# An attention and feed-forward layer: context stored as 256 plain rows, value products of two steps next to each other, and a new order of work inside a round

## The chip, the cores and the metric

The kernel runs on one core of one Trainium2 chip. The metric is the device time in microseconds (us). Three runs of the kernel before took 2249.22, 2251.18 and 2252.72 us; the median is 2251.18 us.

The core has a matrix engine (PE, with PEld for its weight loads), a vector engine (DVE), a scalar engine (ACT), a general engine (POOL) and a sequencer that issues transfers (SP). Each has its own queue and runs it in order; semaphores tie them together.

## The reference

One layer of a transformer: batch 2, sequence 2048, width 256, 16 heads of 16, relative position embeddings clipped at distance 64, then a feed-forward part of width 704 whose activations and weights are rounded to a 4-bit grid in blocks of 16.

```python
B, S, D, H, R = (2, 2048, 256, 16, 64); HD = 16
dist = jnp.clip(idx[None, :] - idx[:, None], -R, R) + R
pe_k, pe_v = rel_emb_k[dist], rel_emb_v[dist]
q, k, v = qkv[0], qkv[1], qkv[2]              # from layernorm(x) @ W_qkv + b_qkv
score = einsum('bhqd,bhkd->bhqk', q / sqrt(hd), k) + einsum('bhqd,qkd->bhqk', q / sqrt(hd), pe_k)
attn = softmax(score)
ctx = einsum('bhqk,bhkd->bhqd', attn, v) + einsum('bhqk,qkd->bhqd', attn, pe_v)
x = x + ctx @ W_out + b_out
xq = fp4(layernorm(x)); h = silu(xq @ fp4(w_gate).T) * (xq @ fp4(w_up).T)
x = x + fp4(h) @ fp4(w_down).T
```

## The kernel before

**Stages.** `projections` makes queries, keys and values, `attention` does the rounds, `ffn_weights` transposes the weights of the last part, and `ffn` does the output projection and the feed-forward part, 32 tiles of 128 tokens.

**A round.** The attention part is 32 rounds (`iteration`): 8 groups of 4 heads times 4 blocks of 512 queries. A round has 16 steps. Each step has a string in `ORDER`, and every engine walks the same strings and does its share of each letter:

- `S`: one half of a score unit, 128 keys by 512 queries of one head, into one of 4 PSUM banks (`psS`). PE makes it (steps 0 and 1: `near_half`, with four transposes L925 and four products L932; later steps: `far_half` L943), ACT takes the exponential (L1084, L1089).
- `M`: one product of the search for each query's maximum, one or two rounds ahead (PE L845, into one of 3 banks of `psA`); DVE reduces it (L1139). There are 64 in a round. The last three steps of a round already hold those of the round after next (`AHEAD`, 11 of them).
- `V`: the value products of one step (`far_values` L863): four heads, each on its own 32 columns of the array, fp32, summed in `psC`. In step 2 it is `band_values` (L955). A `V` works on the step before it; the last step's is done at the start of the next round.
- `P`, `F`: relative positions for the values (L968, then DVE L1179, then L980). `P` needs POOL's `mix_band` (L798, L804), which starts when `band_values` is done.
- `R`, `X`: the relative scores of the next round (PE L852, ACT L1076, DVE L1144, POOL `widen_rel` L790). When the fourth is widened, SP writes them out and reads them back skewed (`rel_skew`, then `rel_near`).
- `T`: the negated maxima of the next round are transposed (L871), ACT copies them (L1068), POOL cuts them in three (`cut_shift` L778 to L784) and SP puts them beside the queries (`queries<-shift`, L717). In a round at an end of the sequence (qb 0 and 3) POOL first clears an edge of `rel_near` (L772).
- `D`, `B`: the end of the last round. ACT copies `psC` (`copy_context` L1056, at the start of step 1), PE transposes the sums (`denominators` L879), DVE inverts them (L1160), ACT widens the inverses (L1063), PE transposes them back (`turn_back` L887, four transposes), DVE multiplies (`normalise` L1167) and SP stores the context in 32-row strips per head (L722).

**Slots.** `probs` has four slots: the exponentials of two steps. The exponential of step s waits until the value product of step s-2 is done.

**After the rounds.** The value bias and the first row of the relative values are not in the values; `ffn_weights` works them, and the output bias, into spare rows of `w_out_rows` (taps: DVE L1714 to L1718, PE L1748, DVE L1726). In `ffn` each tile's output projection is four fp32 products (`project` L1432), each recorded twice. PE's order for tile n is gate and up product of n+1, down product of n-1, projection of n+5, transposes of x of n+2 and of h of n. DVE follows the strings `ODD` and `EVEN` with the operations of h (`H`), of x (`X`, one pair of tiles every two tiles) and of the output (`Y`).

Of the kernel before, what the change touches and what calls it, by code (L numbers as in the profile page):

```python
# [30 lines left out]
P = 128  # L31
# [24 lines left out]
VWIDE = 32  # L56

# [59 lines left out]
def projections(nc, c, x, w_qkv, b_qkv, rel_k, rel_v, dr, io):  # L117
# [13 lines left out]
    with ExitStack() as ctx:  # L131
        def sb(name, shape, dt=F32):
            return ctx.enter_context(nc.sbuf_tensor(name, shape, dt))

        (w_in, x_in, b_in, passed, ln_stats, ln_var, ln_std, ln_rstd, ln_done, p_dve, xt_ready, xt_copied,
# [3 lines left out]
            "w_in x_in*2 b_in passed ln_stats ln_var ln_std ln_rstd ln_done p_dve xt_ready xt_copied "  # L139
# [17 lines left out]
        prt = sb("rel_prt", [HD, 3, P], BF16)  # L157
        rv = sb("rv_rows", [P, 2, HD])
# [72 lines left out]
        def _(sp):  # L231
# [22 lines left out]
            sp.dma_start(w[:], w_qkv.rearrange("(c p) n -> p c n", p=P)).then_inc(w_in, 16)  # L254
            with nc.allow_non_contiguous_dma("small tables, once"):
                sp.dma_start(bcol[:], b_qkv[0:2 * D].rearrange("(t p) -> p t", p=P)).then_inc(b_in, 16)
                sp.dma_start(relT[:], rel_k.rearrange("r d -> d r")).then_inc(k_dma, 16)
            sp.dma_start(rv[:, 0, :], rel_v[0:1, :].broadcast_to([P, HD])).then_inc(k_dma, 16)
# [75 lines left out]
        def _(dve):  # L334
# [32 lines left out]
            def values(n):  # L367
# [3 lines left out]
                for i in range(CH):  # L371
                    dve.wait_ge(v_ready, n * (CH // 2) + i // 2 + 1)
                    src = psV[:, i, :].rearrange("p (h d) -> p h d", h=H)
                    if i:
                        v.tensor_copy(vheads[:, t0 + CH * j + i, :, 0:HD], src).then_inc(v_taken, 1)
                    else:
                        v.tensor_copy(vheads[HALF:P, t0 + CH * j, :, 0:HD], src[HALF:P]).then_inc(v_taken, 1)
                        v.tensor_copy(vheads[0:HALF, t0 + CH * (j + 1) % KT, :, 0:HD], src[0:HALF]).then_inc(v_taken, 1)

            def relative_tables():  # L380

                dve.wait_ge(k_dma, 16 * 4)
                ch.mark(v.tensor_sub(vd[:, 0, :], rvt[:], rv[:, 0, :]))
                ch.link(v.tensor_sub(vd[:, 1, :], rvt[:], rv[:, 1, :]))
                dve.sem_inc(k_rel, 1)
# [9 lines left out]
            def masks():  # L395
# [3 lines left out]
                ch.link(v.tensor_reduce(c.head[:], c.ident[:].rearrange("p (h c) -> p h c", h=HG)[:, :, 0:HD], AX.X, ALU.add))  # L399
# [13 lines left out]
            dve.wait_ge(b_ready, 2)  # L413
            for n in range(N):
# [73 lines left out]
class Dram:  # L488


    def __init__(self, nc):
# [7 lines left out]
        self.ctx = d("ctx_d", [B * KT, P, HG, P])  # L499


class Consts:
    def __init__(self, nc, ctx):
# [6 lines left out]
        self.head = sb("head_rows", [P, HG])  # L510
# [31 lines left out]
RSTEPS = (4, 5, 6, 7)  # L542

ORDER = (
    "MSMVMMSMSMMSM", "SMSMMSMSDM", "SMMSSMVMSMB", "VSMSSMMS",
    "SMSMSSMVRM", "MSMSMSSXMRV", "XSSMMSSMVRM", "SMSMSSMVRXM",
    "SSMSMXSVP", "MSVSMSMSM", "SMSSSMVF", "MMSMSVMSS",
    "SMMSMSVMS", "SSMSVMST", "MMSSMSVMSMM", "SSMVMSSM",
)
RATE = tuple(x.count("M") for x in ORDER)  # L550
# [12 lines left out]
def score_slots():  # L563
# [3 lines left out]
    def add(*key):  # L567
        slots[key] = len(slots)
# [4 lines left out]
    for it in range(LAST + 1):  # L573
        for step in range(STEPS):
            half = 0
            for kind in ORDER[step]:
# [3 lines left out]
                elif kind == "R" and it < LAST:  # L580
                    add("R", it + 1, RSTEPS.index(step))
# [18 lines left out]
def emptied(*key):  # L600

    return SCORE[key] + 1 + SBANKS

# [38 lines left out]
def attention(nc, c, dr, io, fw):  # L642
    with ExitStack() as ctx:
        def sb(name, shape, dt=F32):
# [5 lines left out]
         shift_ready, ctx_copied, rden_wide,  # L650
# [4 lines left out]
            "shift_ready ctx_copied rden_wide "  # L655
# [4 lines left out]
        probs = sb("probs", [P, 4, 2, NQ])  # L660
# [5 lines left out]
        rwide = sb("rden_wide", [P, NQ])  # L666
# [4 lines left out]
        rden = sb("rden", [P, NQ])  # L671
# [25 lines left out]
        def _(sp):  # L697
# [21 lines left out]
            def store_context(g, qb):  # L719

                wait_alone(sp, passed, small_taken, taken("B", g * QB + qb))
                sp.dma_start(ctx_rows(g, qb), rden[:].rearrange("p (i t) -> p i t", i=CH)).then_inc(ctx_out, 16)  # L722

            def iteration(g, qb, before=None, last=False):
# [14 lines left out]
                if it == 1:  # L739
                    sp.wait_ge(w_set, 4)  # L740
# [4 lines left out]

            def ctx_rows(g, qb):
                b, gg = g // NG, g % NG
                return dr.ctx[bass.ds(b * KT + qb * CH, CH), :, gg, :].rearrange("i p t -> p i t")
# [12 lines left out]
            wait_alone(sp, passed, ctx_out, 16 * (GRP * QB + 1))  # L761
# [29 lines left out]

# [1008 lines left out]
```

## Time and profile before

| | |
|---|---|
| median of three runs | 2251.18 us |
| the profiled execution | 2251.05 us |
| its span, first to last instruction | 2249.2 us |
| PE busy | 2174.0 us (97%) |
| DVE busy | 1868.9 us (83%) |
| ACT busy | 1349.4 us (60%) |
| POOL busy | 676.4 us (30%) |
| mean granted clock of PE | 0.979 of full |

Stages by the trace: projections to about 123 us; the first maxima to 171; the rounds to about 1873; the last context to 1877; the weights to 1890; the feed-forward part to 2249. PE's busy share is near full in both long stages. The share alone does not say whether PE sets the pace: the matrix products overlap, and their ends are modelled. What an engine really takes is read from the distance between the starts of two instructions when nothing was waited for.

### The profile page before, as it was taken

The page shows a single profiled execution, that of the slowest core. Times are in us where ns is not written, and L with a number is a line of the kernel's source. Part 1 is how long each engine was busy: PE and PEld are TensorE (multiplying, and loading weights), DVE is VectorE, ACT ScalarE, POOL GpSimd, SP SyncE. Part 2 cuts the span into 40 slices and gives each one's busy share as a digit, 9 for nine tenths or more (in the row PEclk, how much of TensorE's full clock was granted, in tenths as well). Part 3 has the DMA queues.
Part 4 walks back from the last instruction along what each step waited for, and adds up shares of the span by engine and source line. Part 5 has one row for each costly group of instructions (what it writes and reads, how often), then busy time and mean ns, then how long its engine had stood idle before and what let it go on. Part 6 is the DMA issues. An engine that isn't in the chain of part 4 may idle for free. (4 is left out here: it accounts for less than half of the span.)

```text
span 2249.2 us, 50086 instructions
## 1 busy us (share of the span) xinstructions
PE 2174.0 (97%) x20396; PEld 1139.1 (51%) x20396; DVE 1868.9 (83%) x3408; ACT 1349.4 (60%) x2544; POOL 676.4 (30%) x484
## 2 busy tenths in 40 slices
PE   7989999999999999999999999999999996999998
PEld 3524444554444444444444444545444443677775
DVE  6787888888888888888888888888888833899997
ACT  3406766767677777676776766766677773233332
POOL 5503333333333333333333333333333330011111
PEclk9958999999999999999999999999999998999999
DMA  5743433343333333433443333343333221111100
GB/s 162 192 115 92 137 98 88 102 106 91 98 103 98 88 97 98 114 105 102 110 112 98 98 98 98 96 105 98 92 89 88 81 81 63 38 57 54 50 33 17
DMA packets 275178, 210.74 MB, mean 94 GB/s; under 512 B 16642, under 2 KB 266116, under 8 KB 274820
## 3 DMA queue, kind: packets, MB, share of 16 engines
q1 hardware_dynamic: 273796, 203.34, 32.9%
q0 software_dynamic: 1152, 4.19, 0.6%
q8 instruction: 161, 2.64, 0.5%
q14 instruction: 69, 0.57, 0.1%
HBM read 113.35 MB, written 93.34 MB: 92 GB/s over the span
## 5 line engine op out<-in xcount | busy, mean ns | idle before, releaser
L1139 DVE TENSOR_REDUCE amax<-psA 128x1 f32<-128x512 f32 x2048 | 1297.2, 684 | 203.6 <-PE psA L845 190.3
L1089 ACT ACTIVATE probs<-psS 128x512 f32<-128x512 f32 x1792 | 943.3, 609 | 337.4 <-PE psS L943 333.0
L845 PE MATMUL psA<-keys,queries 96*128 96x512 bf16 x2048 | 737.4, 390 | 2.0 <-DVE amax L1139 2.0
L943 PE MATMUL psS<-queries,keys 102*128 102x512 bf16 (+7 forms) x2176 | 586.1, 342 | 0.7
L863 PE MATMUL psC<-probs,vals 128*32 128x512 f32 (+7 forms) x4352 | 475.7, 524 | 3.9 <-ACT probs L1089 2.2
L798 POOL TENSOR_TENSOR band_probs<-band_probs,side 128x2048 f32<-128x2048 f32 x64 | 288.9, 4535 | 494.2 <-PE psC L955 494.2
L845 PEld LDWEIGHTS psA<-keys,queries 96*128 96x128 bf16 x2048 | 190.7, 98 | 336.6 <-DVE amax L1139 224.3
L943 PEld LDWEIGHTS psS<-queries,keys 102*128 102x128 bf16 (+1 forms) x2176 | 203.2, 98 | 213.4 <-ACT probs L1089 46.8
L1084 ACT ACTIVATE band_probs<-psS 128x512 f32<-128x512 f32 x256 | 153.6, 601 | 131.9 <-PE psS L932 131.8
L863 PEld LDWEIGHTS psC<-probs,vals 128*32 128x32 f32 (+1 forms) x4352 | 89.2, 102 | 197.0 <-ACT probs L1089 111.8
L1452 PE MATMUL psG<-w_gate_up_T,f_xqT 128*128 128x352 f32 x512 | 161.9, 471 | 0.5 <-ACT f_xqT L1508 0.5
L925 PE MATMUL psS<-ident,rel_near 128*128 128x128 f32 x1024 | 156.4, 275 | 0.0
L925 PEld LDWEIGHTS psS<-ident,rel_near 128*128 128x128 f32 x1024 | 129.6, 142 | 35.4 <-ACT band_probs L1084 1.1
L804 POOL TENSOR_TENSOR band_probs<-band_probs 128x2048 f32<-128x2048 f32 x32 | 145.2, 4537 | 5.7 <-POOL band_probs L798 2.9
L1391 POOL TENSOR_TENSOR f_hq<-f_h_grid,f_h_scale 128x704 f32<-128x704 f32 x32 | 44.4, 1388 | 305.3 <-DVE f_h_grid L1627 305.3
L1452 PEld LDWEIGHTS psG<-w_gate_up_T,f_xqT 128*128 128x128 f32 x512 | 97.6, 196 | 51.1 <-issue 4.5
L932 PE MATMUL psS<-queries,keys 99*128 99x128 bf16 (+1 forms) x1024 | 100.5, 220 | 9.0 <-DMA queries<-shift 8.7
L1076 ACT COPY rel_scores<-psS 128x512 f32<-128x512 f32 x128 | 75.5, 593 | 52.0 <-PE psS L852 52.0
L778 POOL CAST shift<-shift_res 32x128 bf16<-32x128 f32 x32 | 9.1, 284 | 310.8 <-ACT shift_res L1068 310.8
L772 POOL MEMSET rel_near<- 128x256 f32 x16 | 5.1, 317 | 303.1 <-DMA rel_near<-rel_skew 303.1
L1472 PE MATMUL psD<-w_down_T,f_hqT 128*128 128x256 f32 x384 | 89.9, 385 | 1.9 <-ACT f_hqT L1516 1.9
L790 POOL COPY rel_scores<-rel_scores 128x512 f32<-128x512 f32 x128 | 78.0, 638 | 36.1 <-ACT rel_scores L1076 36.1
(164 smaller groups left out, 1923.7 us busy)
## 6 DMA issues: line engine op xcount, KB each, us to landing
rel_skew<-rel_scores SPq DMA_DIRECT2D x32, 2048.0 KB, 9.1
rel_near<-rel_skew SPq DMA_DIRECT2D x64, 1024.0 KB, 8.1
keys<-k_ring SPq DMA_DIRECT2D x48, 256.0 KB, 5.7
queries<-q_parts SPq DMA_DIRECT2D x192, 64.0 KB, 2.4
ctx_d<-rden SPq DMA_DIRECT2D x32, 256.0 KB, 2.3
ctx_in<-ctx_d SPq DMA_DIRECT2D x16, 512.0 KB, 3.9
q_parts<-parts SPq DMA_DIRECT2D x16, 384.0 KB, 3.1
k_ring<-parts SPq DMA_DIRECT2D x12, 384.0 KB, 3.3
```

Source lines behind the costliest of these rows:

```text
L798: p.tensor_mul(both, both, c.side[:, e, None, :].broadcast_to([P, APAIRS, P])).then_inc(side_cut, 1)
L804: p.tensor_add(band[:, 0].rearrange("p h u q -> p (h u q)"), band[:, 0].rearrange("p h u q -> p (h u q)"), band[:, 1].rearrange("p h u q - ...
L845: t.matmul(small("M", m, n), qs[0:NR, qb, h, u * P:(u + 1) * P], keys[0:NR, par, h, c0:c0 + NQ], start=True, stop=True).then_inc(small_rea ...
L863: ins = t.matmul(psC[32 * h:32 * h + v.shape[1], q0:q0 + k], v, probs[:, n % 4, h % 2, o:o + k], start=False, stop=False, skip_group_check ...
L925: t.matmul(bank[:, u * P:(u + 1) * P], near[:, h * CH + u, e, :], c.ident[:], start=(u == 0), stop=False, is_transpose=True, skip_group_ch ...
L932: ins = t.matmul(bank[:, u * P:(u + 1) * P], keys[0:nr, par, h, c0:c0 + P], qs[0:nr, qb, h, u * P:(u + 1) * P], start=False, stop=(u == CH ...
L943: ins = t.matmul(bank[:, o:o + k], keys[0:nr, par, h, c0:c0 + P], qs[0:nr, qb, h, q0:q0 + k], start=True, stop=True, skip_group_check=True)
L1084: ins = a.activation(band[:, e, 2 * c2 + half].rearrange("p u q -> p (u q)"), src, ACT.Exp)
L1089: ins = a.activation(probs[:, n % 4, half], src, ACT.Exp)
L1139: v.reduce_max(amax[:, pair, k:k + 1], small("M", m, n), AX.X).then_inc(small_taken, 1)
L1452: ins = t.matmul(psG[:, half, 0:GU], xqT[:, m % 4, cc, :], wgu[:, cc, half * GU:(half + 1) * GU], start=(cc == 0), stop=(cc == 1))
L1472: ins = t.matmul(psD[:, 0:D], hqT[:, m % 2, f, :], wd[:, f, :], start=(f == 0), stop=(f == FT - 1))
```

## The change

- **Order.** `ORDER` is a new table. Value products are no longer tied to the step before: `value_order` lists them, two (steps 14 and 15) go over to the next round, and `VV` puts two next to each other. `probs` has eight slots.
- **Context.** DVE divides straight from the transposed sums (`scale`), POOL adds the part of the last relative row (`add_ends`), PE turns the result back with two transposes, DVE copies it (`take_turned`), and SP stores plain rows, 16 per head, in two transfers. `widen_inverses` is gone. ACT's copy has a letter of its own, `C`.
- **Biases.** The value bias and the first relative row are added to the values in `projections`; the output bias is added to x by POOL in `ffn` (`add_bias`). The taps are gone.
- **Projection.** Two products per tile instead of four.

```diff
 ORDER = (
-    "MSMVMMSMSMMSM", "SMSMMSMSDM", "SMMSSMVMSMB", "VSMSSMMS",
-    ... twelve more
+    "MMVVMSMMSMMSMMSC", "SMSMDSMSM", "SMSSSMM", "SSMVMSMSM",
+    ... twelve more
 )
+PROBS = 8
+CARRIED = 2
+def value_order(it):
+    left = [(it - 1, step) for step in range(STEPS - CARRIED, STEPS)] if it else [None] * CARRIED
+    return left + [(it, BAND_STEPS - 1)] + [(it, step) for step in range(BAND_STEPS, STEPS - CARRIED)]
...
+            def add_ends(it):                                  # POOL, between cut_shift and mix_band
+                wait_alone(pool, passed, small_taken, taken("D", it))
+                p.tensor_mul(ended[:], scaled[:, :, HD + 1:HD + 2].broadcast_to([P, APAIRS, HD]),
+                             c.ends[:, None, :].broadcast_to([P, APAIRS, HD])).then_inc(ends_added, 1)
+                ...
+                p.tensor_add(rows[:], scaled[:, :, 0:HD], ended[:]).then_inc(ctx_rows_ready, 1)
...
             def turn_back(it):
-                pe.wait_ge(rden_wide, it + 1)
+                pe.wait_ge(ctx_rows_ready, it + 1)
                 slot_free("B", it)
-                for u in range(CH):
+                for j in range(2):
                     ...
-            pe.sem_inc(pv_done, 2)
+            pe.sem_inc(pv_done, PROBS // 2)
...
-            def widen_inverses(it):
...
-            def invert(it):
+            def scale(it):
                 ready("D", it)
+                v.reciprocal(rcol[:], sums[:, :, HD]).then_inc(inverted, 1)
+                ...
+                v.tensor_mul(scaled[:], sums[:, :, 0:HD + 2], rcol[:, :, None].broadcast_to([P, APAIRS, HD + 2])).then_inc(small_taken, 1)
-            def normalise(it):
-                v.tensor_mul(rden[:], ctxs[:], small("B", it)).then_inc(small_taken, 1)
+            def take_turned(it):
+                v.tensor_copy(turned[:].rearrange("p j t -> p (j t)"), small("B", it)[:, 0:2 * P]).then_inc(small_taken, 1)
...
+            def add_bias(p):                                   # POOL in ffn
+                pool.wait_ge(r_in[k], 16 * (p // 2 + 1))
+                nc.gpsimd.tensor_add(both, both, bo[:, None, :].broadcast_to([P, 2, D])).then_inc(res_ready, 1)
+            add_bias(0)
+            add_bias(1)
             for n in range(NT):
+                if n % 2 == 0 and n // 2 + 2 < NP:
+                    add_bias(n // 2 + 2)
                 pool.wait_ge(hs_ready, n + 1)
...
-                for g in range(NG):
-                    ins = t.matmul(psO[...], cx[:, p % 2, half, g, :], wo[:, g, :], ...)
+                for cc in range(D // P):
+                    ins = t.matmul(psO[...], cx[:, p % 2, half, cc, :], wo[:, cc, :], ...)
...
-            pe.wait_ge(w_copied, 3 * KD)                       # ffn_weights
+            pe.wait_ge(w_free, KD)
```

PE's queue in the middle of a round before, around step 8 (`psA<-keys,queries` is an M, `psS<-queries,keys` an S, `psC<-probs,vals` a V, `tv` is P):

```order
L943 MATMUL psS<-queries,keys 128x512
L863 MATMUL psC<-probs,vals 32x512 x4
L968 MATMUL psA<-band_probs,tv 32x32 x64
L845 MATMUL psA<-keys,queries 128x512
L943 MATMUL psS<-queries,keys 128x512
L863 MATMUL psC<-probs,vals 32x512 x4
L943 MATMUL psS<-queries,keys 128x512
```

The same work now, in step 11:

```order
L886 MATMUL psA<-keys,queries 128x512
L984 MATMUL psS<-queries,keys 128x512
L886 MATMUL psA<-keys,queries 128x512
L904 MATMUL psC<-probs,vals 32x512 x8
L1009 MATMUL psA<-band_probs,tv 32x32 x64
L984 MATMUL psS<-queries,keys 128x512
L886 MATMUL psA<-keys,queries 128x512 x2
```

A block of 32-column products (V, P, F) that stood apart now often holds two or three of them: `x8` is two value products in a row. The positions moved from step 8 to step 11, the fold from step 10 to 12. In a whole round there were 15 such blocks and there are 11: by steps, before 0, 2, 3, 4, 5, 6, 7, 8 (V P), 9, 10 (V F), 11, 12, 13, 14, 15; now 0 (V V), 3, 4, 6, 7, 8 (V V), 10 (V V), 11 (V V P), 12 (F V), 13, 15. The band's products moved from step 2 to 3, `D` stayed in step 1 and `B` went from step 2 to 4; the last `R` went from step 7 to 8, `T` from the end of step 13 to the middle of 14. `AHEAD` is now 9.

POOL's queue for one round before (cut of the shift, mixing of the band, widening of the relative scores):

```order
L784 TENSOR_TENSOR shift<-shift_res,shift 32x128
L798 TENSOR_TENSOR band_probs<-band_probs,side 128x2048 x2
L804 TENSOR_TENSOR band_probs<-band_probs 128x2048
L790 COPY rel_scores<-rel_scores 128x4x128 x4
L778 CAST shift<-shift_res 32x128
```

and now:

```order
L811 TENSOR_TENSOR shift<-shift_res,shift 32x128
L823 TENSOR_TENSOR ctx_ends<-ctx_scaled,rel_v_ends 128x256
L828 TENSOR_TENSOR ctx_rows<-ctx_scaled,ctx_ends 128x256
L836 TENSOR_TENSOR band_probs<-band_probs,side 128x2048 x2
L842 TENSOR_TENSOR band_probs<-band_probs 128x2048
L817 COPY rel_scores<-rel_scores 128x4x128 x4
L805 CAST shift<-shift_res 32x128
```

Two operations on the context of the round before stand ahead of the mixing.

## Rows read from the trace of the kernel before

**Rows 1.** The page, part 1: busy time, share of the span, instructions of each engine.

```profile
PE 2174.0 (97%) x20396; PEld 1139.1 (51%) x20396; DVE 1868.9 (83%) x3408; ACT 1349.4 (60%) x2544; POOL 676.4 (30%) x484
```

**Rows 2.** Windows: stretch, its length, busy time (instructions) by engine, clock, DMA share, GB/s.

```profile
600.00:1600.00 1000.00, 996.90 (x10978) 485.96 (x10977) 869.73 (x1503) 699.26 (x1333) 336.78 (x226) 1.00 0.37 100
1827.00:1873.00 46.00, 42.14 (x504) 18.96 (x504) 1.64 (x3) 34.10 (x66) 14.12 (x4) 0.96 0.03 7
2000.00:2200.00 200.00, 199.74 (x866) 149.84 (x865) 192.98 (x405) 67.07 (x110) 26.50 (x20) 1.00 0.14 45
```

**Rows 3.** Source line L871, once a round: ns min/median/max, first and last start.

```profile
L871 PE MATMUL psS<-ident,negm x32: 272/273/421, 171.6 to 1820.4; 128*32 128x128 f32 x32
```

**Rows 4.** Timeline of PE, two stretches of one round: start us, us, line, operation.

```profile
1005.59 1.05 PE L863 MATMUL psC<-probs,vals 128*17 128x512 f32 x8
1006.46 1.42 PE L968 MATMUL psA<-band_probs,tv 128*32 128x32 f32 x128
1007.81 0.39 PE L845 MATMUL psA<-keys,queries 96*128 96x512 bf16 x1
1008.03 0.38 PE L943 MATMUL psS<-queries,keys 99*128 99x512 bf16 x1
1008.34 1.05 PE L863 MATMUL psC<-probs,vals 128*17 128x512 f32 x8
1009.33 0.39 PE L943 MATMUL psS<-queries,keys 99*128 99x512 bf16 x1
...
1037.22 0.61 PE L879 MATMUL psA<-ident,ctx_sum 128*128 128x128 f32 x4
1037.66 0.38 PE L845 MATMUL psA<-keys,queries 96*128 96x512 bf16 x1
```

**Rows 5.** Groups by line: busy us, mean ns, idle before and its releasers.

```profile
L1139 DVE TENSOR_REDUCE amax<-psA 128x1 f32<-128x512 f32 x2048 | 1297.2, 684 | 203.6 <-PE psA L845 190.3
L804 POOL TENSOR_TENSOR band_probs<-band_probs 128x2048 f32<-128x2048 f32 x32 | 145.2, 4537 | 5.7 <-POOL band_probs L798 2.9 <-ACT rel_scores L1076 2.5 <-POOL band_probs L802 0.4
L1635 DVE TENSOR_TENSOR f_y<-psD,x 128x256 f32<-128x256 f32 x32 | 13.3, 416 | 10.5 <-PE psD L1472 10.5
```

**Rows 6.** Timeline of DVE before the first round.

```profile
127.33 38.34 DVE L1139 TENSOR_REDUCE amax<-psA 128x1 f32<-128x512 f32 x64
```

**Rows 7.** Timeline of POOL and PE around the turn of two rounds.

```profile
1024.47 0.32 POOL L772 MEMSET rel_near<- 128x256 f32 x1 [18.88 <-DMA rel_near<-rel_skew]
1028.86 0.39 PE L932 MATMUL psS<-queries,keys 102*128 102x128 bf16 x4
1058.17 0.62 POOL L790 COPY rel_scores<-rel_scores 128x512 f32<-128x512 f32 x1 [0.44 <-ACT rel_scores L1076]
```

**Rows 8.** Timeline of the weights' stage and the first projections.

```profile
1879.42 4.82 PE L1733 MATMUL psW<-ident,w_rows 128*128 128x128 f32 x24 [3.46 <-PEq L643]
1885.40 1.53 PE L1741 MATMUL psW<-ident,w_rows 128*128 128x128 f32 x12 [1.16 <-DVE w_gate_up_T L1723]
1888.77 1.22 DVE L1726 TENSOR_TENSOR w_out_rows<-w_out_rows,psW 128x1024 f32<-128x1024 f32 x1 [3.42 <-PE psW L1748]
1893.96 5.29 PE L1432 MATMUL psO<-w_out_rows,ctx_in 128*128 128x256 f32 x16 [5.30 <-DMA ctx_in<-ctx_d]
```

**Rows 9.** Timeline of two tiles of the feed-forward part.

```profile
2059.76 1.39 POOL L1391 TENSOR_TENSOR f_hq<-f_h_grid,f_h_scale 128x704 f32<-128x704 f32 x1 [8.27 <-DVE f_h_grid L1627]
2062.23 0.68 DVE L1560 TENSOR_TENSOR f_x_tmp<-f_xn,f_x_scale 128x512 f32<-128x512 f32 x1
2069.85 1.89 PE L1432 MATMUL psO<-w_out_rows,ctx_in 128*128 128x256 f32 x8
2071.85 0.69 DVE L1579 TENSOR_TENSOR x<-psO,x_res 128x512 f32<-128x512 f32 x1 [0.35 <-PE psO L1432]
```

**Rows 10.** Source line L1557, the inverse scales of x: ns min/median/max.

```profile
L1557 DVE TENSOR_SCALAR f_x_scale<-f_x_scale x16: 180/990/992, 1903.9 to 2202.6; 128x32 f32<-128x32 f32 x16
```

**Rows 11.** The page, part 6: transfers, KB each, median us from issue to landing.

```profile
x_res<-in_L_attn_x SPq DMA_DIRECT2D x16, 256.0 KB, 4.2
```

More of the change, by code:

```diff
@@ L509, in __init__ @@
         self.mask_q = sb("mask_q", [P, 2])
[L510 removed]
+        self.ends = sb("rel_v_ends", [P, HD])
         self.fold = sb("fold", [P, 4, 32])
@@ L670, in attention @@
         ctxs = sb("ctx_sum", [P, NQ])
-        rden = sb("rden", [P, NQ])
+        scaled = sb("ctx_scaled", [P, APAIRS, HD + 2])
+        ended = sb("ctx_ends", [P, APAIRS, HD])
+        rows = sb("ctx_rows", [P, APAIRS, HD])
+        turned = sb("ctx_turned", [P, 2, P])
         psS = ctx.enter_context(nc.psum_tensor("psS", [P, SBANKS, NQ], F32))
@@ L995, in iteration @@
                             if not ends:
-                                rel_products(it + 1, qb1, RSTEPS.index(step))
+                                rel_products(it + 1, qb1, next(rel_heads))
                         elif kind == "P":
@@ L1009, in iteration @@
                                 turn_maxima(it + 1)
-                        elif kind != "V":
-                            continue
-                        elif step == 0:
-                            if not first:
-                                far_values(gp, qp, STEPS - 1)
-                        elif step == 2:
-                            band_values()
-                        else:
-                            far_values(g, qb, step - 1)
+                        elif kind == "V":
+                            work = next(values)
+                            if work == (it, BAND_STEPS - 1):
+                                band_values()
+                            elif work is not None:
+                                far_values(work[0] // QB, work[0] % QB, work[1])
                 if ends:
-                    far_values(g, qb, STEPS - 1)
+                    for step in range(STEPS - CARRIED, STEPS):
+                        far_values(g, qb, step)
                     denominators(it)
                     turn_back(it)
-            pe.sem_inc(pv_done, 2)
+            pe.sem_inc(pv_done, PROBS // 2)
             pe.wait_ge(keys_in, KDMAS * 16)
@@ L1094, in iteration @@
                 ends = last and qb == QB - 1
+                rel_heads = iter(range(RUNITS))
                 for step in range(STEPS):
-                    if step == 1 and not first:
-                        copy_context(it - 1)
                     half = 0
                     for kind in ORDER[step]:
-                        if kind == "S":
+                        if kind == "C" and not first:
+                            copy_context(it - 1)
+                        elif kind == "S":
                             exponentials(it, 2 * step + half // 2, half % 2)
                             half += 1
-                            if step == 2 and half == 2 and not first:
-                                widen_inverses(it - 1)
                         elif kind == "R" and not ends:
-                            copy_rel(it + 1, RSTEPS.index(step))
+                            copy_rel(it + 1, next(rel_heads))
                         elif kind == "T" and not ends:
@@ L1197, in iteration @@
                         elif kind == "X" and not ends:
-                            rel_maxima(it + 1, RSTEPS.index(step - 1))
+                            rel_maxima(it + 1, next(rel_heads))
                         elif kind == "P":
@@ L1699, in _ @@
         def _(sp):
[L1700 to L1703 removed]
+            sp.dma_start(wo[:], w_out.rearrange("(c p) n -> p c n", p=P)).then_inc(o_in, 16)
+            sp.dma_start(bo[:], b_out[None, :].broadcast_to([P, D])).then_inc(o_in, 16)
+            sp.wait_ge(o_in, 32)
         @block.vector
```

186 lines of the change are left out of this document (86 added, 100 removed).

## The prediction

> **What bounds the kernel now.** I read the page's busy shares first [rows 1]: PE 97%, DVE 83%. The windows [rows 2] then show who is full in each long stage: PE 996.9 of 1000 us in the rounds, at full clock, DVE 870; in the feed-forward part PE 199.7 of 200 and DVE 193.0. A modelled share proves little, so I added up one round from distances between starts. L871 stands once in a round, and its 32 starts go from 171.6 to 1820.4 us [rows 3]: 1648.8 / 31 = 53.19 us per round. From the timeline of PE [rows 4]: an M or S takes 0.22 us (1007.81 to 1008.03); four fp32 transposes 0.44 (1037.22 to 1037.66); a V in the middle of a block 0.87 (1005.59 to 1006.46); P at the end of one 1.35, 1.22 of it its own. From an S before a lone V to the product after it are 1009.33 - 1008.03 = 1.30 us, 0.22 of it the S: a lone V costs 1.08. So each block pays 0.21 us once, at its ends. A round: 64 M and 56 far S at 0.22 (0.2166 over long stretches) 26.0; 8 near S at 0.66 5.3; 4 R 0.9; 14 V at 0.87 12.2; the band's products (64, about 1.8), P and F (about 1.2 each) 4.2; D and B 0.9; T 0.1; 15 blocks at 0.21 3.2. Sum 52.8, against 53.19: 0.4 us of a round are waits, the rest is PE's own work. PE bounds the rounds, and work taken off it comes off the time.
>
> DVE in a round: an M costs it 38.34 / 64 = 0.60 us at full pace [rows 6], so 64 take 38.4; with X, P, the maxima and the weights' operations it comes to about 46, and it waits 190 us for M's in all [rows 5]. It has 6 us to spare per round.
>
> **Part by part.** The profiled execution took 2251.05 us (span 2249.2, 1.85 around it), the median is 2251.18: the sum is made against 2251.05.
>
> 1. Fewer blocks. 15 become 11: 4 x 0.21 = 0.84 us a round. The price of a neighbour is seen (V to P 0.87); two V's that sum into the same `psC` are not, and could save nothing or the whole 0.21. I take 0.21, since the band's 64 products sum into `psC` too and fill it at their own pace.
> 2. `turn_back` two transposes instead of four: 0.22.
>  Together 1.06 us. Rounds 1 to 30: 31.8 us. Round 0 has neither carried V's nor a B, and 14 blocks become 10: 0.8.
> 3. DVE per round: gone are the inverse (0.26) and the product of 512 columns (0.69, as x<-psO [rows 9]); new are the inverse, a product of 288 columns and a copy of 256 (0.42, as L1635 [rows 5]). About +0.2 us, hidden under the 6 us. ACT loses a copy of 0.6 us; it had a third of its time free. POOL gets two operations of 256 columns: 4.54 us for 2048 columns [rows 5] gives 0.57 each, before `mix_band`, while POOL waits for the band's products anyway. B needs them only in step 4, some 8 us later.
> 4. Where M's lie close: step 0 issues two M's and then seven after VV, 2 x 0.87 + 0.21 = 1.95 us in which DVE empties its banks; the seven need 7 x 0.60 = 4.2 us and PE takes 3.5 us over them, with three banks in between. In step 8 DVE has 4.7 us of work in PE's 4.1, in step 9 2.2 in 1.3, in steps 10 to 12 9.9 in 12.6. It evens out within the banks and two steps; I take the waits of 0.4 us per round as unchanged (0 to 1.0 new).
> 5. Before the first round PE and DVE do 64 + `AHEAD` M's at DVE's 0.60, and T waits for all. Two fewer: 1.2 us. They come back in round 30 at PE's 0.22: +0.4.
> 6. The last round has no M's. It lasted 1827.5 to 1873.0, 45.5 us, PE busy 42.1 and ACT 34.1 of 46 [rows 2]. Far value products waited for the exponentials of the step just before, and P for POOL: P follows the band's products by 14 us of mixing. Now P comes three steps later and a V has slack of a step or more. PE's own work in it is about 39 us; ends 39 and 46. I take 42: 3.5 us.
> 7. The end of that round is bare: ACT's widening (0.62), two transposes and the shorter last DVE operation go, 1.1 us; DVE's product (0.45), POOL's two operations and the wait between them (1.4) and a second transfer issue come. +1.1 us.
> 8. Weights. PE's last transposes waited to 1885.40 for DVE's copies, and the stage ended with DVE's sum, 1888.77 + 1.22 = 1889.99 [rows 8]. Now they wait for ACT's copies alone, which are done before the first 24 transposes end (1884.24). They start 1.2 us earlier and nothing but ACT's copies of w_down follows: end near 1886.7. The w_out transfer is issued first and fits in. 3.3 us.
> 9. First projections: 16 records in 5.29 us [rows 8] become 8, 2.65 us off a path on which DVE waits. The bias sum on POOL needs x, which lands 4.2 us after its issue near 1890.7 [rows 11], and then 1.1 us: 1896.1, against PE's end at 1896.6. Hidden by 0.5 us; it costs what it is later if the context lands sooner.
> 10. Feed-forward, two tiles. PE issues 16 projection records of 0.215 less 8: 1.7 us less of 20.3. But DVE follows closely: in 20.3 us its only wait is 0.35 us before x<-psO [rows 9], where PE's projection ends. DVE then bounds. 14 pairs x 0.35 = 4.9 us, and no more.
> 11. The bias sum `add_bias` on POOL, 512 columns, 1.13 us by the rate of L804 [rows 5]. L1557 lasts 180 ns alone and 990 in the median [rows 10], and ends when POOL's product of h ends: DVE's operations between SBUF tiles wait for POOL's. The sum runs right behind the product, 2061.15 to about 2062.35; DVE's next operation with both inputs in SBUF, L1560, starts at 2062.23 [rows 9]. It loses 0.1 to 0.2 us a pair: 14 x 0.15 = 2.1. The third sum falls into DVE's bare chain for the first tiles: up to 1.1, I take 0.9.
>
> The Trainium skill (SBUF — State Buffer, "Who interferes with whom") says that a DVE instruction with two SBUF inputs contends with a GpSimd instruction that reads SBUF, and that the loser fully blocks. With the 990 ns of L1557 beside 180 the trace agrees on blocking. By that rule POOL's sum in its turn could be blocked by DVE; nothing waits for it for 15 us, so the sum stays.
>
> Projections: one DVE sum more at the start (0.4 us) while DVE waits 4.9 us for PE; the sums into the values take the place of copies of the same size (0.42). 0, at most 0.5.
>
> Sum: -31.8 - 0.8 - 1.2 + 0.4 - 3.5 + 1.1 - 3.3 - 2.65 - 4.9 + 2.1 + 0.9 = -43.7. 2251.05 - 43.7 = **2207.4 us**, 1.9% less.
>
> **Rivals.**
>
> A. *Neighbouring V's save nothing.* Each of two V's still costs 1.08. For it: no two V's stand together in the trace. Against: V to P is 0.87. Then 31 rounds keep 0.84: +26.0, 2233.4 us. Chance 0.07.
>
> B. *DVE sets the pace in places.* The M's bunch more than the three banks carry, and PE waits in steps 8 and 9 and after VV. For it: 4.7 us of DVE work in 4.1. Against: 6 us free per round. Half a microsecond a round gives 2223, one a round 2238. Chance 0.10.
>
> C. *POOL's sums hold up DVE in the feed-forward part.* If each pair loses the whole 1.1 us and not 0.15: 14 x 1.0 = +13.3, 2220.7 us. It would need DVE's order to put an SBUF operation at once behind the product of h. Chance 0.06.
>
> D. *Slower: the skewed scores come late in the edge rounds.* A chain runs beside every round: the last R, ACT, POOL's widening (done at 1058.79, 30.6 us into its round), transfers out and back, in a round at an end of the sequence the clearing of the edge, then the cut of the shift, three transfers, and PE's first L932. The edge was cleared at 1024.47 and L932 started at 1028.86 [rows 7], 4.4 us later and about 0.7 us into its round: it ends just as PE wants it. The round before began near 975.0 (53.19 us earlier), so the edge came 49.5 us into it. Now the band's products are 1.8 us later, and with them POOL's mixing and widening, which then ends about 0.8 us later. The edge comes near 50.3, the shift near 54.7, and PE wants it at 52.1 + 3.0 = 55.1, since VV, three M's and four transposes go first: 0.4 us to spare. If transfers or POOL take d longer, the 15 edge rounds after the first each lose d - 0.4. With d = 4 us that is 54 us: 2207.4 + 54 = 2261 us; from d = 3.3 us the kernel is slower. For it: the slack was about nothing before. Against: no transfer of the chain carries more, and POOL's two new operations lie in a gap of its own. Chance 0.05, 0.04 of it slower and 0.01 level.
>
> **How the numbers follow.** The forecast 0.72, with its own range 2197 to 2217 (0.4 us of waits gone in each round at one end, new waits of 0.3 at the other). A 0.07, B 0.10, C 0.06, D 0.05. Range for 8 in 10: 2196 to 2226; it takes in C and half of B. A measurement of this kernel tells a change from none at about 0.2%, 4.5 us. Faster: all but D, 0.94, less 0.01 for something unseen: 0.93; level 0.03, slower 0.04.
>
> **What would show it.** Starts of the transposed maxima 52.1 us apart (A: 52.9, B: 52.6 to 53, D: PE waiting for queries<-shift at the turn). From the first V of a VV to the second 0.87. In the feed-forward part 20.33 - 0.35 = 19.98 + 0.15 = 20.1 us per pair, PE idle about 1.5 of them, and L1560's successor longer than 0.68. The last round 42 us, with P not waiting. From its last copy of the context to the first projection 19 us, where it was 21. Wrong if PE's busy time in the rounds falls and the round's length does not, or if DVE's idle before M goes to zero.

## The result, and the profile after

The changed kernel takes 2289.57 us in the median (2284.88 to 2293.99, 4 runs), the kernel before 2250.59 on the same chip: ratio 1.0172, 95% interval 1.0150 to 1.0195. It is slower by 39 us, where 44 us less was forecast.

The page, part 1, of the changed kernel, which answers to [rows 1]:

```profile
PE 2146.0 (94%) x20196; PEld 1123.5 (49%) x20196; DVE 1920.4 (84%) x3426; ACT 1308.3 (57%) x2512; POOL 737.9 (32%) x564
```

PE has 200 instructions fewer and is busy 28 us less, as the change meant, and still the span is 34 us longer (2283.1). DVE has 18 instructions more and is busy 51.5 us more: 2.9 us for each new one, though none of the new ones in a round lasts over 0.5. So old instructions had become longer.

The windows of the changed kernel (stretch, its length, busy time and instructions of PE, PEld, DVE, ACT, POOL, granted clock, DMA share, GB/s; compare [rows 2]) say in which stage, and the source line of the transposed maxima (ns min/median/max, first and last start; compare [rows 3]) says how much:

```profile
600.00:1600.00 1000.00, 962.06 (x10454) 471.41 (x10452) 874.64 (x1470) 652.39 (x1273) 343.32 (x253) 0.98 0.34 95
2000.00:2200.00 200.00, 188.63 (x805) 138.48 (x804) 196.41 (x412) 67.89 (x112) 40.05 (x30) 1.00 0.13 41
L912 PE MATMUL psS<-ident,negm x32: 269/273/421, 170.5 to 1871.7; 128*32 128x128 f32 x32
```

PE is full no longer in the rounds, and its clock is 0.98 where it was 1.00. A turn is one start of this line, once a round. From turn to turn it takes (1871.7 - 170.5) / 31 = 54.88 us; before it was 53.19, and 52.1 was forecast. The 31 distances tell more than the mean: the last is 51.2, eight others are 51.7 to 52.3, as forecast, and the rest go up to 59.3. So the change does what it should in a round of its own, and something else hits some rounds. The longer page groups (busy us, mean ns, idle before and its releasers; compare [rows 5]) name the wait:

```profile
L886 PE MATMUL psA<-keys,queries 96*128 96x512 bf16 x2048 | 729.9, 392 | 51.1 <-DVE amax L1169 50.5
L842 POOL TENSOR_TENSOR band_probs<-band_probs 128x2048 f32<-128x2048 f32 x32 | 144.9, 4529 | 6.0 <-ACT probs L1121 2.7
```

PE waits 50.5 us before M's for DVE to empty a bank. In the kernel before that wait was 2.0. What does DVE do meanwhile? The timelines of one long round of the changed kernel, step 7, of DVE and of POOL (start us, us, engine line, operation):

```profile
1016.82 3.23 DVE L1169 TENSOR_REDUCE amax<-psA 128x1 f32<-128x512 f32 x5
1019.96 4.14 DVE L1288 TENSOR_TENSOR w_tmp<-w_tmp,w_bits 128x256 f32<-128x256 f32 x1
1024.02 1.88 DVE L1169 TENSOR_REDUCE amax<-psA 128x1 f32<-128x512 f32 x3
```

```profile
1009.43 9.01 POOL L836 TENSOR_TENSOR band_probs<-band_probs,side 128x2048 f32<-128x2048 f32 x2 [3.31 <-PE psC L996]
...
1019.30 4.51 POOL L842 TENSOR_TENSOR band_probs<-band_probs 128x2048 f32<-128x2048 f32 x1 [0.18 <-ACT probs L1121]
```

L1288 is one of the ten small operations per row of weights (`weight_ops`) that DVE slips in, one in each of the steps in `WSTEPS`, 7 to 12, in both kernels. It works on 256 columns and lasts 0.41 us when nothing holds it up (the least of 16 is 406 ns). Here it starts 0.66 us into POOL's sum of the two mixed bands and ends at 1024.10, 0.3 us after the sum. PE in the same round:

```profile
1020.26 1.07 PE L904 MATMUL psC<-probs,vals 128*32 128x384 f32 x16
1021.26 0.39 PE L886 MATMUL psA<-keys,queries 96*128 96x512 bf16 x1
1021.49 0.38 PE L984 MATMUL psS<-queries,keys 99*128 99x512 bf16 x1
1024.76 0.39 PE L886 MATMUL psA<-keys,queries 96*128 96x512 bf16 x1 [2.89 <-DVE amax L1169]
...
1026.55 3.59 PE L904 MATMUL psC<-probs,vals 128*17 128x512 f32 x16
...
1032.57 1.91 PE L904 MATMUL psC<-probs,vals 128*17 128x512 f32 x16
```

The three banks of `psA` cover about 1.2 us of the 4.1; then PE stands for 2.89. The price does not end there: the next pair of V's takes 3.59 us where one later in the same round takes 1.91. The window over it, same columns as above, shows why:

```profile
1026.50:1030.10 3.60, 3.60 (x18) 0.52 (x18) 2.71 (x5) 1.07 (x3) 0.62 (x1) 0.53 0.34 123
```

The granted clock is 0.53 over it, which is nearly all at the lower of the two levels (1.2 GHz), after PE had stood. Between the first turn and the last PE stood 16 times for 2.1 to 2.9 us in this way: ten operations to a row of weights, six of them in a round, so in three rounds of five step 7 gets one of the kinds that are held up. With 13 of the 16 the clock records show the lower level for 3.41 or 6.83 us, beginning 1.7 to 4.8 us after PE had stopped (in three cases before it ran again): 61.4 us in all. In the kernel before they show none between the first turn and the last. If what runs in such a stretch takes twice as long, about 30 us were lost (an estimate, half of 61.4), beside 48.5 us of waits for DVE.

The rounds bear that estimate out. Set against the same round of the run without the collision (`e1_late_weights`, below), a round with such a stall is longer than by the stall itself: by 0.5 us in the mean of the 3 where the clock stayed up, by 2.2 in the 8 with 3.41 us of the lower clock and by 4.0 in the 5 with 6.83. The differences, 1.7 and 3.5 us, are half of the stretches.

Why now, and not before? The same place in the kernel before, rows not yet shown (DVE, then POOL; the round of [rows 7]):

```profile
1055.12 1.03 DVE L1241 TENSOR_TENSOR w_tmp<-w_rows,w_scale 128x256 f32<-128x256 f32 x1
```

```profile
1051.34 4.53 POOL L804 TENSOR_TENSOR band_probs<-band_probs 128x2048 f32<-128x2048 f32 x1 [0.18 <-ACT rel_scores L1076]
```

There step 7's weight operation began 0.75 us ahead of the end of the sum (1055.87) and ended 0.28 behind it. It was already held up, by 0.6 us, which the banks covered. The change moved the two towards each other. In these two rounds, counted from the first M of step 0 (1028.20 before, 994.45 now), the sum ends at 29.4 us where it ended at 27.7, and the weight operation of step 7 starts at 25.5 where it started at 26.9. POOL mixes later because the band's products do: ahead of the mixing it stands 3.31 us for them (the row of L836 above), so its two new operations, which come before that wait, delay nothing. Some 3 us of shift, and a wait of 0.6 us became one of 3.7.

### The profile page after: what moved, and what is told of

Read it like the earlier page. It is cut to its first block and busy times, and to the rows that moved or that the text cites. A ratio compares the mean times of both kernels' runs of the same rounds, so it can differ in the third digit from the quotient of the medians.

```text
span 2283.1 us, 49869 instructions
## 1 busy us (share of the span) xinstructions
PE 2146.0 (94%) x20196; PEld 1123.5 (49%) x20196; DVE 1920.4 (84%) x3426; ACT 1308.3 (57%) x2512; POOL 737.9 (32%) x564
## 5 line engine op out<-in xcount | busy, mean ns | idle before, releaser
L886 PE MATMUL psA<-keys,queries 96*128 96x512 bf16 x2048 | 729.9, 392 | 51.1 <-DVE amax L1169 50.5
L984 PE MATMUL psS<-queries,keys 102*128 102x512 bf16 (+7 forms) x2176 | 592.4, 344 | 1.9
L904 PE MATMUL psC<-probs,vals 128*32 128x512 f32 (+7 forms) x4352 | 469.9, 540 | 1.7 <-issue 1.6
L836 POOL TENSOR_TENSOR band_probs<-band_probs,side 128x2048 f32<-128x2048 f32 x64 | 288.7, 4535 | 118.2 <-PE psC L996 118.2
L904 PEld LDWEIGHTS psC<-probs,vals 128*32 128x32 f32 (+1 forms) x4352 | 107.9, 105 | 221.2 <-issue 124.0
L823 POOL TENSOR_TENSOR ctx_ends<-ctx_scaled,rel_v_ends 128x256 f32<-128x256 f32 x32 | 20.6, 643 | 328.6 <-DVE ctx_scaled L1195 328.6
```

The lines of the kernel that those rows point to most:

```text
L836: p.tensor_mul(both, both, c.side[:, e, None, :].broadcast_to([P, APAIRS, P])).then_inc(side_cut, 1)
L886: t.matmul(small("M", m, n), qs[0:NR, qb, h, u * P:(u + 1) * P], keys[0:NR, par, h, c0:c0 + NQ], start=True, stop=True).then_inc(small_rea ...
L904: ins = t.matmul(psC[32 * h:32 * h + v.shape[1], q0:q0 + k], v, probs[:, probs_slot(g * QB + qb, n), h % 2, o:o + k], start=False, stop=Fa ...
L984: ins = t.matmul(bank[:, o:o + k], keys[0:nr, par, h, c0:c0 + P], qs[0:nr, qb, h, q0:q0 + k], start=True, stop=True, skip_group_check=True)
```

## The experiments

The theory (P): an operation of DVE of the kind of L1276, L1282 and L1288 waits until POOL's sum ends, PE runs out of banks and then loses clock. The rival (B of the prediction): M's lie too close for three banks, and DVE sets the pace. Every edit below is against the changed kernel unless it says otherwise.

**e1_late_weights.**

```
-WSTEPS = range(7, 13)
+WSTEPS = range(10, 16)
```

> The changed kernel with one number changed: DVE's weight operations (one per step) stand in steps 10 to 15 of a round and not in 7 to 12. Theory P (POOL blocks DVE): in the changed kernel a weight operation with two inputs in SBUF, or a tensor_scalar, is issued just after POOL has begun the 4.5 us sum of the band and waits for its end; DVE then frees no bank, PE stands about 3 us, and sometimes its clock falls afterwards. In steps 10 to 15 POOL is idle or copies: every round takes about 52.1 us, 31 x (54.88 - 52.1) = 86 us less, about 2204 us. Theory B (the maxima products are bunched more than DVE and three banks can carry in step 8): only 0.4 us of DVE work leaves step 8, rounds stay above 54, about 2277 us or more.

Measured: 2197.02 us (2196.61 to 2198.12), ratio 0.9772 (0.9757 to 0.9786). One line gives back 93 us, and the kernel is 2.3% faster than the one before. The M's stand in the same order as before, and rounds above 54 us, which B expected, are gone. The turns are (1784.1 - 170.5) / 31 = 52.05 us apart:

```profile
L912 PE MATMUL psS<-ident,negm x32: 269/273/421, 170.5 to 1784.1; 128*32 128x128 f32 x32
L1276 DVE TENSOR_TENSOR w_tmp<-w_rows,w_scale x16: 412/416/517, 326.4 to 1629.2; 128x256 f32<-128x256 f32 x12, 128x352 f32<-128x352 f32 x4
L886 PE MATMUL psA<-keys,queries 96*128 96x512 bf16 x2048 | 725.1, 390 | 3.9 <-DVE amax L1169 2.4
```

**e2_short_mix.** It leaves the weights where they were and takes away the other partner: POOL's sum is made over 32 columns only.

```
-p.tensor_add(<2048 columns of band 0>, <band 0>, <band 1>)
+p.tensor_add(band[:, 0, 0, 0, 0:32], band[:, 0, 0, 0, 0:32], band[:, 1, 0, 0, 0:32])
```

> The changed kernel with POOL's last operation on the band (the sum of its two halves, 2048 columns, 4.5 us) cut to 32 columns; the rest of the sum is left out. Weight operations stay in steps 7 to 12. Theory P: the operation that DVE waited behind is gone, the two before it end ahead of step 7; rounds 52.0 to 52.5 us, the whole 2200 to 2215 us. Theory B: nothing changes for DVE, 2285 to 2290 us.

Measured in one run: 2199.55 us. Either partner taken away gives the same 2197 to 2200. Here DVE's weight operations stay in steps 7 to 12, so its load there is what it was, and PE's waits for it are gone all the same: that refutes B. POOL's mask products (L836 in the changed kernel, 9 us for two) remain, and the longest of the first weight product (L1275 here) was 0.96 us: the sum was the partner that mattered.

```profile
L1275 DVE TENSOR_TENSOR w_tmp<-w_rows,w_scale x16: 410/423/961, 316.0 to 1620.7; 128x256 f32<-128x256 f32 x12, 128x352 f32<-128x352 f32 x4
L885 PE MATMUL psA<-keys,queries 96*128 96x512 bf16 x2048 | 723.5, 390 | 3.4 <-DVE amax L1168 2.3
```

**e3_before_early_weights.** If P holds, the kernel before must fall ill when only its weight operations move one step towards the sum.

```
 (the kernel before)
-WSTEPS = range(7, 13)
+WSTEPS = range(6, 12)
```

> The kernel before with its weight operations in steps 6 to 11 and not 7 to 12. Its step 6 begins about 22.6 us into the round, POOL's sum of the band runs from about 22.9 to 27.4. Theory P: in three rounds of five the operation of step 6 is of a kind that waits, 16 stalls of about 3 us and some clock: 2290 to 2320 us. Theory B: the old order is as it was, 2250 us.

Measured: 2330.35 us (2326.31 to 2334.64), ratio 1.0358 (1.0341 to 1.0375). That is above the expected 2290 to 2320. The old kernel is ill in the same way and worse: turns 55.85 us apart, PE standing 16 times for 2.35 to 3.17 us, the lower clock with every one of them, 75 us in all, and

```profile
L1253 DVE TENSOR_TENSOR w_tmp<-w_tmp,w_bits x16: 412/866/4275, 374.2 to 1781.9; 128x256 f32<-128x256 f32 x12, 128x352 f32<-128x352 f32 x4
```

**e4_before_late_weights.** The other way, steps 10 to 15 in the kernel before.

> The kernel before with its weight operations in steps 10 to 15. It shows what the old order is worth without any meeting on the port. Theory P: the few short waits of before (an operation of 0.42 us that took 1.06) go, its longer rounds of 53.4 to 54.5 us fall to 52.9: about 8 us less, 2242 us. Theory B: 2250 us.

Measured: 2248.52 us, ratio 1.0001 (0.9992 to 1.0011). The long weight operations are gone (L1241: 412/415/516 ns) and nothing is gained. The expectation missed: waits of up to 0.65 us in that operation had been covered by the banks, and the old kernel's long rounds (53.4 to 54.2) have another cause. For the two longest the trace names it, PE's waits of 1.20 and 1.07 us for `queries<-shift` (1.47 and 1.25 in the kernel before); for the others it stays open. The run also shows that e1's gain over the old kernel is the change's own, not the move's.

**e9_half_sum and e10_steps_8_13.** Two doses. The first halves POOL's sum (1024 of 2048 columns), the second moves the weight operations by one step.

```
-WSTEPS = range(7, 13)
+WSTEPS = range(8, 14)
```

> The changed kernel (2289.57 us) with POOL's sum of the two mixed bands (L842) cut to half of its columns, 1024 of 2048 for each head pair's slot together (the other half of the sum is left out); the weights' operations stay in steps 7 to 12. The sum lasts about 2.26 us in place of 4.53 and begins at the same time. Theory: the weight operation waits until the sum ends, so the longest shrink from 4.1 to about 1.9 us; the idle time of 2.9 us before the sixth M of the step shrinks to about 0.6, too short to bring the granted clock down: 2197 + 16 x 0.6 = about 2207 us. If the wait were a fixed price of an operation beside POOL, or the theory were wrong, it would stay near 2290 or fall by less than a third.

> The changed kernel (2289.57 us) with the weights' operations in steps 8 to 13 in place of 7 to 12. Step 8 begins about 2.5 to 3 us after step 7, and POOL's sum ends 4.8 us after step 7 began. Theory: the operation in step 8 meets the last 1.5 to 2 us of the sum, its longest is about 2 us, TensorE idles under 1 us in 16 rounds and the clock stays up: 2200 to 2210 us. Rival (any weight operation within the mixing costs the same wherever it falls, since the mask's products of POOL, 9 us before, do so too): 2250 or more.

Measured: 2215.73 us (2214.86 to 2219.57) and 2209.63 us (2206.89 to 2211.41). Line L1288 in e9, then L1276 in e10 (ns min/median/max):

```profile
L1288 DVE TENSOR_TENSOR w_tmp<-w_tmp,w_bits x16: 406/462/2001, 366.1 to 1684.8; 128x256 f32<-128x256 f32 x12, 128x352 f32<-128x352 f32 x4
```

```profile
L1276 DVE TENSOR_TENSOR w_tmp<-w_rows,w_scale x16: 410/466/1835, 321.3 to 1635.4; 128x256 f32<-128x256 f32 x12, 128x352 f32<-128x352 f32 x4
```

The wait is what is left of POOL's instruction and no fixed price: 2.17 us less of sum (2.36 for 4.53) made the longest 2.14 us shorter. PE's wait for DVE between the turns fell from 48.5 to 9.5 and 9.3 us, and the clock was not down once. e10 is at the upper end of its expectation and e9 is 9 us above: its rounds grew by 17.7 us against e1's (52.63 - 52.05 a turn) for 9.1 us more of those waits. Another 5.1 us are longer waits of PE ahead of F, which also needs DVE's work; in e10 it is 13.4 us in all, 8.8 for M's and 3.6 ahead of F. So counting PE's waits before M's alone makes a held-up DVE too cheap. That F waits for the delayed DVE is argued, not shown: the profile names no releaser there.

```profile
L886 PE MATMUL psA<-keys,queries 96*128 96x512 bf16 x2048 | 725.4, 390 | 12.0 <-DVE amax L1169 11.5
L886 PE MATMUL psA<-keys,queries 96*128 96x512 bf16 x2048 | 723.4, 390 | 11.7 <-DVE amax L1169 11.2
```

(The whole kernel in e9, then in e10; 9.5 and 9.3 are between the turns.)

**e5_split.** Based on e1, as all that follow. The pairs VV of steps 0, 8, 10 and 11 are pulled apart by one letter.

```
-    "MMVVMSMMSMMSMMSC", ... "SMMXSRXMSVVSMM", ... "SMVVSMSXMSM", "SMVVPSMMSSM",
+    "MMVMVSMMSMMSMMSC", ... "SMMXSRXMSVSVMM", ... "SMVSVMSXMSM", "SVMVPSMMSSM",
```

> The kernel with the weights' operations in steps 10 to 15 (2197.02 us), with the four double V's of ORDER (steps 0, 8, 10, 11) pulled apart, one other letter between them, so that each round has four more blocks of value products and nothing else. Item 1 of the prediction (a block that follows a neighbour costs 0.87 us where one alone costs 1.08): four blocks x 0.21 = 0.84 us per round, x 31 = +26 us, near 2223 us; mean time from turn to turn 52.05 -> 52.9. Rival A (neighbours save nothing): 2197, within 0.2%.

Measured: 2235.85 us (2233.91 to 2237.80). 39 us more, where 26 were expected. By its profile the first turn came 4.3 us later, which no block explains: in the profiles of e3, e4, e5, e8 and e9 the first turn comes at 173.2 to 174.7 us, and all five show 3.41 us of lower clock that begin at 65 to 68 us; in the others it comes at 170.1 to 171.6, and they show none there. The rest is 53.19 - 52.05, 1.13 us a round, or 0.28 for each of the four blocks. Most rounds are 1.0 us longer, 0.25 a block, and five of them by 2 to 3. Rival A is refuted, and item 1 was rather too small.

**e6_proj_twice.** Every output projection is computed twice, four products per tile.

```
-for cc in range(D // P):
+for cc in (0, 1, 0, 1):
```

> The kernel with the weights' operations in steps 10 to 15 (2197.02 us), with each output projection computed a second time (four products per tile, as before the change, the second pair overwriting the first). It undoes item 10 of the prediction alone. If the projection's products stand on the path in the FFN as item 10 said, 32 tiles x 0.153 us = about +5 us (2202), and the stretch from the first x1 to the last (L1622) grows from 287.8 to about 292.7 us. If TensorE waits there for DVE or POOL anyway, under 1 us: 2197 to 2198.

Measured: 2209.08 us (2207.40 to 2211.17), 12 us more. From the first x1 (L1622) to the last 295.5 us where e1 took 287.8, so 7.7 us for item 10, where 4.9 were forecast; by the spans the rest lies mostly between the last turn and the first x1 (72.9 us for 68.0). Of these 4.9 us, 3.3 lie between the first projection and the first x1 (6.3 us for 3.1), where item 9 has its place with 2.65; the other 1.6 come before any of the products that the edit adds, and have another cause. Both items were real, and item 10 larger than forecast.

**e7_small_bias.** POOL's `add_bias` on 2 columns of each tile.

```
-both, both, bo[:, None, :].broadcast_to([P, 2, D])
+both[:, :, 0:2], both[:, :, 0:2], bo[:, None, 0:2].broadcast_to([P, 2, 2])
```

> The kernel with the weights' operations in steps 10 to 15 (2197.02 us), with POOL's addition of the output bias cut to 2 columns of each tile (the rest of the bias is left out). It takes away item 11's work on POOL, 1.27 us for each pair of tiles, in the FFN. Item 11 (2.1 us for 14 of them on the path, by the probabilities' quantised h coming late, and 0.9 for single ones): 2194 us. Rival C (POOL's additions hold up DVE): up to 1.27 x 16 = 20 us less, 2177. If POOL's work there is hidden: 2197.

Measured: 2196.80 us (2196.54 to 2199.14): the columns of the bias sum on POOL cost nothing. Item 11 put 3.0 us on it, and rival C more.

**e8_x_first.** In the feed-forward part the same wait is seen once a pair: L1600 (L1557 in [rows 10]) lasts 990 ns beside POOL's product of h. The operation is moved ahead of that product, by giving the odd tile 12 `X` and the even one 7, and `add_bias` is asked for one pair earlier.

```
-FIRST_X, LAST_X = 13, 6
-ODD, EVEN = "HYXHXXHXXHXHHHHXXHXXHXXX", "HYXHXHXHXHXHXHHHH"
+FIRST_X, LAST_X = 12, 7
+ODD, EVEN = "HYXHXXHXXHXHHHHXXHXXHXX", "HYXXHXHXHXHXHXHHHH"
 ... (the calls of add_bias, moved)
```

> The kernel with the weights' operations in steps 10 to 15 (2197.02 us), with one operation of the x chain moved from the odd tile's turn to the even tile's in the FFN (12 and 7 in place of 13 and 6), and POOL's bias additions one pair earlier, behind the quantised h of the even tile. In the trace DVE's small scale operation of the x chain (L1600) took about 0.8 us more in each pair, behind POOL's product for the quantised h. If this wait is on the path (the blocking theory, as in the rounds): 14 x 0.8 = about -11 us, 2186. If DVE is not what bounds the FFN, 2197 within 2 us.

Measured: 2189.58 us (2186.62 to 2190.34), ratio 0.9733 (0.9718 to 0.9747), the fastest of all. In e1, then in e8:

```profile
L1600 DVE TENSOR_SCALAR f_x_scale<-f_x_scale x16: 181/990/994, 1856.7 to 2148.6; 128x32 f32<-128x32 f32 x16
```

```profile
L1601 DVE TENSOR_SCALAR f_x_scale<-f_x_scale x16: 170/172/180, 1859.8 to 2143.4; 128x32 f32<-128x32 f32 x16
```

The wait of 0.8 us is gone in every pair. The rounds of e8's profile began 3.3 us later (173.8 for 170.5) and the span is 7.9 us shorter, so from the first turn to the end 11.2 us went, the 14 x 0.8 expected. In the median the kernel gained 7.4. Two things moved at once here; since e7 found no price for the bias sum, I put the gain down to the moved operation.

## Why the prediction was wrong

**The step that failed is the last sentence of item 4**, with what item 3 says of DVE: "I take the waits of 0.4 us per round as unchanged (0 to 1.0 new)", with DVE's extra time "hidden under the 6 us". PE's waits for DVE were 48.5 us in the rounds, and the lower clock after them cost some 30 more. I added up DVE's work by durations of one trace and let it even out over two steps. What I did not ask is whether those durations hold once POOL's `mix_band` and DVE's weight operations change places. Item 3 was right that POOL's two new operations before `mix_band` are harmless, because POOL waits there anyway. But rival D had worked out that the band's products, and with them the mixing, come 1.8 us later, and I used that for the skewed scores alone. The sum did end 1.7 us later and step 7's weight operation came 1.4 us earlier, so that it no longer met the last 0.75 us of the sum but nearly the whole of it. No rival stood for this: all of the 0.04 for a slower kernel was D's, and B, the nearest, went to 2238 us. The rounds were forecast 32 us shorter and came out 52.4 longer, a miss of 85 us. The rest of the sum was 7 us too cautious. Both figures are 1.5 us smaller once the turn's own move is taken out (items 6 to 9).

**The evidence stood in the trace of before.** L1241 there lasts 415 ns in the median and 1064 at most:

```profile
L1241 DVE TENSOR_TENSOR w_tmp<-w_rows,w_scale x16: 415/416/1064, 320.6 to 1651.7; 128x256 f32<-128x256 f32 x12, 128x352 f32<-128x352 f32 x4
```

A maximum of two and a half times the median, on an operation that waits for nobody by the profile, is the trace of a neighbour. I had read exactly this in item 11 for L1557, and applied it to the feed-forward part alone. The Trainium skill (SBUF — State Buffer, "Who interferes with whom") says that a DVE instruction with two SBUF inputs contends with a GpSimd instruction that reads SBUF, over a pair of ports that one of them locks while the other is blocked. The trace agrees for L1276 and L1288, 4.1 us beside 0.41. The same section counts `tensor_scalar` with one SBUF input among the operations that can take that pair. The trace agrees again: L1282 reads one SBUF tile and constants, and lasted up to 4.08 us beside 0.28.

Where the 85 us lie, against e1, which has none of it: the rounds of the changed kernel take 1701.2 us and those of e1 1613.6, 87.6 more. PE's waits for DVE are 48.1 us of it (48.5 less 0.4), the lower clock about 30 by the estimate above. Of the other 9 us, waits ahead of F are 4.7 and ahead of V 1.6; some 3 are not accounted for.

**Item by item.**

- Items 1 and 2 were right, if small: e1's rounds are 52.05 us, for 52.1 forecast. The second V of a pair costs 0.87 or less: a pair takes 1.85 us (1053.27 to 1055.12 in the changed kernel) for 1.95 forecast. e5 gives 0.25 to 0.28 a block where 0.21 was taken.
- Item 5: the first turn comes at 170.5 instead of 171.6 us, -1.1 for -1.2.
- Items 6 to 9: from the last turn to the first x1 it was 79.0 us before (1820.4 to 1899.4) and is 67.8 in the changed kernel (1871.7 to 1939.5), 11.2 less where 8.4 was forecast. But T moved within its round: the last round's first product started 4.7 us after the turn (1825.0) and starts 3.1 after it now (1874.8), so 1.5 us of the gain are no gain, and the rounds, measured from turn to turn, look 1.5 us longer than they are. What is left, 9.7, is near the forecast.
- Item 6 alone: from that first product to the last context copy it was 48.0 us and is 43.7, 4.3 less for 3.5. The 45.5 us of the prediction start at 1827.5, behind a wait of 1.91 us for `queries<-shift` that the last round has no longer. P does not wait in it, as foretold. Items 7 to 9 lie behind that copy: 26.4 us became 21.1, 5.3 less for 4.9, and the first projection starts 18.4 us after the copy, for 19. From it to the first x1 it was 5.40 us and is 2.74, which is item 9's 2.65.
- Item 10 was sound but too small. In the steady part a pair takes 19.91 us (2068.56 to 2088.47) where it took 20.34 and 20.1 was forecast, and DVE waits nowhere before x<-psO there: DVE bounds the stage, as the item says. The step is 0.43 us a pair for 0.35; the rest of e6's 7.7 us lies in the first pairs.
- Item 11 was wrong: e7 shows no cost. L1603, which was to lose 0.1 to 0.2 us a pair behind the sum, keeps its 0.69 (L1560 took 0.68 before). The hold-up among the first tiles did come, once: an operation of x (L1612) lasted 1.63 us where the others of its kind last under 0.7. In e7 it is gone, and the time is the same.
- Rivals A and C are refuted by e5 and e7. B named step 8, where PE did stand, and a wrong cause: e2 leaves DVE's work there and has no stalls. D did not come, and its chain even gained: PE waited for `queries<-shift` only once in the changed kernel, 2.0 us ahead of the first round, where it had waited 6.8 us between the first turn and the last and 1.9 at the last round.

Without the collision, the working holds in the main: e1 is at 2197.02 us for the 2207.4 forecast, at the low end of the range. The 10 us lie about 3 in the rounds and the rest behind them, items 10 and 11 above all.

## What to carry to other kernels

A duration in a trace belongs to what ran beside it. Before a change that moves work between engines, take the min, median and max of each small operation of DVE; a long maximum names a collision that already exists, and the change must be checked for where both partners come to lie, to a microsecond. Operations without a due time, such as the weights here, belong where no long POOL instruction runs; moving them costs one line and was worth 93 us. A stall of PE costs more than itself when the granted clock falls after it.

## What the runs showed of the hardware

- A wait of DVE behind a POOL instruction made an operation of 0.41 us last 4.14, and it lasts as long as the POOL instruction has left (up to 0.6, 1.4, 1.6, 3.7 and 3.9 us in the kernel before, e10, e9, the changed kernel and e3). It hits products, differences and even operations on 16 columns with constants (L1267: 159 ns at least, 1590 at most). Reductions and reciprocals of the same chain in the same steps were never held up. Another round of the changed kernel, DVE and then POOL, shows both kinds within one sum: the reciprocal and the maxima keep their time, the operation behind them ends with the sum, at 415.9.

```profile
412.03 0.24 DVE L1270 RECIPROCAL w_scale<-w_scale 128x16 f32<-128x16 f32 x1
412.19 1.22 DVE L1169 TENSOR_REDUCE amax<-psA 128x1 f32<-128x512 f32 x2
413.75 0.69 DVE L1169 TENSOR_REDUCE amax<-psA 128x1 f32<-128x512 f32 x1 [0.35 <-PE psA L886]
414.36 1.57 DVE L1273 TENSOR_SCALAR w_scale<-w_scale 128x16 f32<-128x16 f32 x1
```

```profile
411.37 4.53 POOL L842 TENSOR_TENSOR band_probs<-band_probs 128x2048 f32<-128x2048 f32 x1 [0.18 <-ACT probs L1121]
```

- The granted clock went to the lower level with 13 of 16 stalls of PE of 2.1 to 2.9 us in the changed kernel and with all 16 of 2.35 to 3.17 us in e3, and in e9 and e10, where between the turns PE's waits for DVE were under 1 us and its longest other one 1.86, not once there. The three stalls without it were 2.10 to 2.24 us long, but others of 2.10 and 2.23 had it, and the kernel before kept its clock over a wait of 3.20 us ahead of its first round:

```profile
176.48 0.61 PE L932 MATMUL psS<-queries,keys 102*128 102x128 bf16 x4 [3.20 <-DMA queries<-shift]
```

So length alone does not decide.
